# Gathering the first slot of key rows one block earlier, into the buffers of the tap products and the gate weights, in a two-layer perceiver kernel

## The chip, the cores and the metric

The kernel runs on one core of a Trainium2 chip. The metric is the device time of one execution in microseconds (us); the median of the runs is compared.

## The reference, cut to what matters

128 query rows `x` (width 256) pass two layers. Layer 0 is a cross-attention over 12,544 context rows with 4 heads, a gated delta rule with 12 heads, and a mixture of 8 experts (top 1). Layer 1 is a second cross-attention over the same context with 16 heads, a linear attention and another mixture (top 2). Each stage adds to `x`, and each starts with a layer norm:

```python
x = x + _L0_xattn_ref(_layernorm(x), ctx_1024, mask, ...)
x = x + _L0_attn_ref(_layernorm(x), ...)          # gated delta rule
x = x + _L0_ffn_ref(_layernorm(x), ...)           # experts, top 1
x = x + _L1_xattn_ref(_layernorm(x), ctx_1024, ...)
x = x + _L1_attn_ref(_layernorm(x), ...)
x = x + _L1_ffn_ref(_layernorm(x), ...)
```

In the second cross-attention scores = (q + bias) k^T / 4 for each of 16 heads of width 16, then a softmax over all context rows, then the product with v. Its keys and values depend on the context alone, not on `x`.

## The kernel before

The program is three blocks, each of which ends with a barrier of all engines. Block 1 (to 448 us) is the first cross-attention over 14 chunks of 896 context rows; beside it the kernel already computes the keys and values of layer 1 for every chunk and stores them in HBM (`kscr`, in two halves of 512 and 384 columns, and `vscr`). Block 2 (448 to 537 us) is the delta rule: `Wc`, `Wg`, `Wo` are its weights, `vpair` (seen as `vp`) holds the products of its convolution taps, ScalarE writes them in `products`, GpSimd adds them up in `add_taps`, and each group of them that is done raises the semaphore `convp` (5 groups). `gate` multiplies by `Wg`, and ScalarE's reading of the product raises `sg` (3 groups). Block 3 (from 537 us) is the experts `moe0`, the second cross-attention (`second_sync`, `second_tensor`, `second_vector`, ...), the linear attention and the last experts `moe1`.

The second cross-attention reads a chunk of keys from SBUF tiles `krows`, a ring of three slots for each of the two halves, 96 partitions wide (and three rows of ones). `gather(sp, c, half)` fills slot `c % 3` with four DMAs from SyncE's queue (L1654). The first two gathers, for chunk 0, stand at the end of the loads that `moe0` issues (`l1_loads`, L1675), behind the weights `lraw`, `dec`, `bg`, `bv1`; `fetch_values` (L1661) and the gathers of chunk 1 (L1785) come behind them.

What TensorE does in block 3 is written out by hand. After the query is ready, four calls of `pick_rows` (L2001) build the query rows in the layout of the keys, and ScalarE copies them (L2131, semaphore `qpicked`). The list `PRO1` is the prologue: 16 scores of chunk 0 and 7 of chunk 1 (`score`, L1904: two matmuls, 512 and 384 columns), among them 14 `late_values` (L1992). The first score waits for both halves of slot 0:

```python
if h == 0:
    for half in range(2):
        pe.wait_ge(S(f"krows{half}_{r}"), 16 * GPARTS * (c // R1 + 1))
```

VectorE takes the maximum of each score (`largest`, L2061) and so frees one of two pairs of PSUM banks, so that a score waits for the maximum of the score two places ahead (`sm_free`). Then comes the loop over 14 chunks, which interleaves transposed scores (L1948), values (L1961) and the scores of the chunk after (L1904); the negated maxima go into the query rows by three small DMAs per chunk (`rows`, L1777).

Of the kernel before, what the change touches and what calls it, by code (L numbers as in the profile page):

```python
# [17 lines left out]
F32 = mybir.dt.float32  # L18
BF16 = mybir.dt.bfloat16
# [5 lines left out]
P = 128  # L25
D = 256
DC = D // P
# [4 lines left out]
HW = (HT[0] * P, HT[1] * P)  # L32
# [6 lines left out]
TWO_ONES = 1.0 + 127.0 / 65536.0  # L39
# [3 lines left out]
H1, D1 = 16, 16  # L43
# [5 lines left out]
KROWS = NJ * D1  # L49
KONES = KROWS + 3  # L50
VW = H1 * (D1 + 1) + D1 - 1

NH, DK, DV = 12, 64, 128
# [3 lines left out]
TAPS = 4  # L57
GH = 4
NG = NH // GH
# [7 lines left out]
def build(nc, a, out):  # L67
# [4 lines left out]
    def S(name):  # L72

        if name not in sems:
            sems[name] = nc.alloc_semaphore(name)
        return sems[name]
# [31 lines left out]
    def sb(st, name, shape, dt=F32):  # L108
        return st.enter_context(nc.sbuf_tensor(name, shape, dt))
# [9 lines left out]
    with ctx:  # L119
        psum = ctx.enter_context(nc.psum_tensor("bank", [P, 8, 512], F32))  # L120
        bank = [psum[:, i, :] for i in range(8)]
# [3 lines left out]
        keep = ctx.enter_context(ExitStack())  # L125
# [60 lines left out]

        home = sb(keep, "home", [P, DC * CB * P])
        eT0 = home[:, 0:DC * E * D].rearrange("p (k e d) -> p k e d", k=DC, e=E)
        gw = ExitStack()
        Wc = home[:].rearrange("p (k o) -> p k o", k=DC)  # L190
        Wg = sb(gw, "Wg", [P, DC, NH * DV])
        Wo = sb(gw, "Wo", [P, NH, D])
        Wgb = sb(gw, "Wgb", [P, DC, 2 * NH])
        convw = sb(gw, "convw", [P, CB, TAPS])
        gbias = sb(gw, "gbias", [P, 2 * NH])
        nA = sb(gw, "nA", [P, NH])
        gnw = sb(gw, "gnw", [P, DV])
        vpair = sb(gw, "vpair", [P, TAPS * 2 * GH * P])

        def load_later_weights(eng, part):  # L200

# [709 lines left out]
            return tile[:, hb(g)].rearrange("p (j e) t -> p e j t", e=2)  # L911

        spent = []
        STILL = ("rms", "og", "on", "oT_psum", "oT", "ew0_in", "e0T_psum", "e0T", "x2_psum", "x2", "vscr_mid", "moe0rw_in")

        with nc.Block(no_gpsimd_drain=True) as block:
            @block.sync
            def _(sp):
                sp.dma_start(ew[:], a["L0_ffn_expert_w"].rearrange("e (c p) d -> p (e c) d", p=P)).then_inc(S("ew0_in"), 16)
                sp.dma_start(rwmoe0[:], a["L0_ffn_router_w"]).then_inc(S("moe0rw_in"), 16)  # L920
                sp.wait_ge(S("v1mid"), CT)
                sp.dma_start(vscr[NCH - 2].rearrange("p t w -> p (t w)"),
                             v1s[:, 0].rearrange("p t w -> p (t w)")).then_inc(S("vscr_mid"), 16)
                sp.wait_ge(S("vscr_mid"), 16)

            @block.vector
            def _(dve):
# [701 lines left out]
        bv1 = sb(xb, "bv1", [P, D])  # L1629
        rd1 = sb(xb, "rd1", [P, H1])  # L1630
        l1 = ExitStack()
        R1, PR = 3, 8
        krows = [sb(l1, f"krows{half}", [KONES, R1, H1, HW[half]], BF16) for half in range(2)]
        v1 = sb(l1, "v1", [P, R1, CT, VW])
        mx1 = sb(l1, "mx1", [P, 2, H1])
        run1 = sb(l1, "run1", [P, 2, H1])
# [7 lines left out]
        HB = P // D1  # L1644
        pickhome = v1[:, 2].rearrange("p t w -> p (t w)")[:, 0:3 * HB * KROWS // 2]
        picks = pickhome.bitcast(BF16).rearrange("p (l k r) -> p l k r", l=HB, k=3)

        GPARTS = 4

        def gather(sp, c, half):  # L1650

            for part in range(GPARTS):
                heads = slice(part * H1 // GPARTS, (part + 1) * H1 // GPARTS)
                sp.dma_start(krows[half][0:KROWS, c % R1, heads].rearrange("r h m -> r (h m)"),  # L1654
                             kscr[half][c].rearrange("j (d h) b m -> (j d) (h b) m", d=D1)[:, heads].rearrange("r h m -> r (h m)")
                             ).then_inc(S(f"krows{half}_{c % R1}"), 16)

        def fetch_values(sp, c):

# [4 lines left out]
        def l1_loads(sp):  # L1664
            o = (0, 6, 8, 10)
            for k, name in enumerate(("L1_attn_Wqkv", "L1_attn_Wout", "L1_attn_Wgate")):
                sp.dma_start(lraw[:, o[k]:o[k + 1]], wcols(a[name], o[k + 1] - o[k])).then_inc(S("lraw_in"), 16)
            dp = a["L1_attn_decay_param"].rearrange("(c h) -> c h", c=DC)
            for c in range(DC):
                sp.dma_start(dec[:, c:c + 1], dp[c].unsqueeze(1).to_broadcast([HL // DC, DL]).unsqueeze(2)  # L1670
                             ).then_inc(S("dec_in"), 16)
            sp.dma_start(bg[:], a["L1_attn_bgate"].rearrange("(c p) -> p c", c=DC),
                         allow_slow_non_contiguous=True).then_inc(S("bg_in"), 16)
            sp.dma_start(bv1[:], a["L1_xattn_bv"].partition_broadcast(P)).then_inc(S("bv1_in"), 16)
            gather(sp, 0, 0)  # L1675
            gather(sp, 0, 1)
            fetch_values(sp, 0)

        def l1_clears(pool):
# [88 lines left out]
        def krow(h):  # L1768

            return h % (P // D1) * DC + h // (P // D1)  # L1770
# [55 lines left out]
        def second_gpsimd(pool):  # L1826
# [35 lines left out]
            value_ones(pool, 2)  # L1862
            pool.wait_ge(S("v1late_ones"), 4)
            pool.wait_ge(S("q3"), 3)
            def ones_rows(half, slots):
                pool.memset(krows[half][KROWS:KONES, slots].rearrange("p s h m -> p (s h m)").bitcast(F32),
                            TWO_ONES).then_inc(S("krows_ones"), 1)
                pool.wait_ge(S("krows_ones"), nth("krows_ones"))

            ones_rows(0, slice(0, 1))  # L1870
            ones_rows(1, slice(0, 1))
            ones_rows(0, slice(1, R1))
            for c in range(NCH):
                maximum(c)
                if c:
                    rescale(c - 1)
                else:
                    pool.wait_ge(S("dm1"), 1)
                    ones_rows(1, slice(1, R1))
                    block_mask()  # L1880
            rescale(NCH - 1)

        def second_tensor(pe):
# [12 lines left out]
            def score(c, h):  # L1896

                r, b = c % R1, sm_bank(("S", c, h))
# [3 lines that stand above are left out]
                sm_free(("S", c, h))  # L1902
                for half in range(2):
                    ins = pe.matmul(bank[b + half][:, 0:HW[half]], qrows[0:KROWS, 0, h, :],  # L1904
                                    krows[half][0:KROWS, r, krow(h), :], start=True, stop=True)
                ins.then_inc(S("sm1"), 1)

            def turn_maximum(c):
# [23 lines left out]
            def scores(c, u):  # L1932

                t, j, g = u // 4, u % 4, UNITS * c + u
                if u == 0:
                    if c == 0:
                        pe.wait_ge(S("krows_ones"), 2)
                    if c == 1:
                        pe.wait_ge(S("krows_ones"), 4)
                        pe.wait_ge(S("qrows_copy"), 16)  # L1940
                    pe.wait_ge(S(f"mrow1_{c % 2}"), 48 * (c // 2 + 1))
                if some(g - 2):
                    pe.wait_ge(S("exp1"), g - 2)
                half = t // HT[0]
                cols = slice((t - half * HT[0]) * P, (t - half * HT[0] + 1) * P)
                for i in range(GH):
                    h = GH * j + i
                    ins = pe.matmul(bank[ST1[g % 3]][:, i * P:(i + 1) * P], krows[half][:, c % R1, krow(h), cols],  # L1948
                                    qrows[:, c % 2, h, :], start=True, stop=True)
                ins.then_inc(S("st1"), 1)  # L1950

# [438 lines left out]
```

## Time and profile before

| | us |
|---|---|
| median of 3 runs | 920.16 (918.53 to 923.98) |
| profiled execution, its own time | 920.66 |
| its span | 918.9 |
| PE busy | 888.6 (97% of the span) |
| VectorE busy | 702.5 (76%) |
| ScalarE busy | 487.3 (53%) |
| GpSimd busy | 301.2 (33%) |
| mean granted TensorE clock | 0.995 of full |

PE is TensorE's matmuls, PEld its weight loads, DVE VectorE, ACT ScalarE, POOL GpSimd, SPq the DMA issues of SyncE. The profiled execution's time is 1.8 us above its span and 0.5 us above the median. PE busy is the share of time with a matmul in flight and does not say that the matmuls run at full rate; the granted clock says at which rate they may run.

### The profile page before, as it was taken

The numbers are of one execution on the slowest core, as the hardware profiler recorded it, in microseconds if no ns is written. First come the engines' busy times: TensorE is split into PE (matmuls) and PEld (weight loads), VectorE is DVE, ScalarE is ACT, GpSimd is POOL, SyncE is SP. The second block draws the span as 40 slices with busy tenths as digits, with TensorE's granted clock in tenths as the row PEclk, the third lists the DMA queues.
The fourth block names the chain that finished last, engine by engine and source line by source line (L and its number), as shares of the span: only waits on it lengthen the run. The fifth ranks groups of instructions, "written<-read, shape, count | busy, mean of one in ns | idle before, by whom it ended". The sixth has DMA issues, their size and how long they took to land. (4 is left out here: it accounts for less than half of the span.)

```text
span 918.9 us, 21566 instructions
## 1 busy us (share of the span) xinstructions
PE 888.6 (97%) x8228; PEld 573.2 (62%) x8228; DVE 702.5 (76%) x1218; ACT 487.3 (53%) x1158; POOL 301.2 (33%) x439
## 2 busy tenths in 40 slices
PE   8999999999999999999899988999999999999898
PEld 5444554555455545665779866667776776776675
DVE  3499888987988898999488655878887888887426
ACT  2543554355345534545297323466766766666753
POOL 5563355336434643566018224500011100000000
PEclk9999999999999999999999998999999999999999
DMA  9467856573556356531410049596666665776100
GB/s 171 173 185 208 261 181 182 142 211 133 141 150 196 104 138 193 165 120 70 145 46 1 2 127 237 153 290 177 185 168 168 168 169 168 181 193 176 47 4 6
DMA packets 115080, 136.35 MB, mean 148 GB/s; under 512 B 65720, under 2 KB 86992, under 8 KB 114992
## 3 DMA queue, kind: packets, MB, share of 16 engines
q1 hardware_dynamic: 111280, 134.23, 52.1%
q10 hardware_dynamic: 3712, 0.92, 0.7%
q8 instruction: 59, 0.97, 0.5%
q14 instruction: 29, 0.24, 0.1%
HBM read 81.48 MB, written 53.07 MB: 146 GB/s over the span
## 5 line engine op out<-in xcount | busy, mean ns | idle before, releaser
L2061 DVE TENSOR_REDUCE mx<-bank 128x1 f32<-128x896 f32 x224 | 233.7, 1085 | 52.6 <-PE bank L1904 49.3
L2122 ACT ACTIVATE p<-bank 128x512 f32<-128x512 f32 x392 | 202.4, 602 | 94.1 <-PE bank L1948 93.9
L721 DVE STREAM_TRANSPOSE ew<-sc 32x896 f32<-32x896 f32 x208 | 229.4, 1103 | 27.7 <-ACT sc L805 20.2
L580 PE MATMUL bank<-Wv,ctxT 128*128 128x512 f32 (+1 forms) x308 | 133.7, 574 | 0.0
L1948 PE MATMUL bank<-home,krows 99*128 99x128 bf16 x1568 | 123.5, 220 | 5.9 <-DMA home<-n3T 2.9
L1904 PE MATMUL bank<-krows,home 96*128 96x512 bf16 x448 | 123.3, 357 | 5.1 <-DMA krows<-kscr 3.7
L1948 PEld LDWEIGHTS bank<-home,krows 99*128 99x128 bf16 x1568 | 99.4, 97 | 43.7 <-issue 8.2
L1961 PE MATMUL bank<-p,v 128*32 128x128 f32 x3136 | 106.8, 276 | 0.9 <-issue 0.9
L1961 PEld LDWEIGHTS bank<-p,v 128*32 128x32 f32 x3136 | 80.1, 109 | 31.3 <-ACT p L2122 27.8
L580 PEld LDWEIGHTS bank<-Wv,ctxT 128*128 128x128 f32 x308 | 58.3, 190 | 65.3 <-issue 58.4
L457 POOL CAST kt<-kf 128x512 bf16<-128x512 f32 (+1 forms) x56 | 31.3, 558 | 202.0 <-ACT kf L777 201.9
L1830 POOL TENSOR_SCALAR neg<-run 128x16 f32<-128x16 f32 x14 | 3.6, 256 | 249.1 <-DVE run L2076 249.1
L777 ACT ACTIVATE kf<-bank,b 128x512 f32<-128x512 f32 (+1 forms) x56 | 35.5, 634 | 86.6 <-PE bank L560 85.6
L560 PE MATMUL bank<-ctxT,WTk 128*128 128x384 f32 (+1 forms) x176 | 75.6, 552 | 0.0
L805 ACT ACTIVATE sc<-sc,neg 128x448 f32<-128x448 f32 x112 | 74.3, 667 | 0.0
L542 PE MATMUL bank<-ctxT,Wk 128*128 128x448 f32 x176 | 70.9, 546 | 0.9 <-ACT kT L765 0.9
L668 DVE CUSTOM_DVE_ANT_0 sc<-bank,pen 128x448 f32<-128x448 f32 x112 | 63.9, 620 | 4.2 <-issue 4.0
L792 ACT COPY v<-bank 128x256 f32<-128x256 f32 x77 | 28.7, 373 | 66.9 <-PE bank L580 66.9
L765 ACT COPY kT<-bank 128x448 f32<-128x448 f32 x56 | 29.7, 532 | 61.6 <-PE bank L542 61.6
L461 POOL TENSOR_TENSOR kf<-kf,kt 128x512 f32<-128x512 f32 (+1 forms) x56 | 58.3, 1041 | 4.4
L463 POOL TENSOR_TENSOR kt<-kf,kt 128x512 bf16<-128x512 f32 (+1 forms) x56 | 58.1, 1038 | 4.4
L459 POOL TENSOR_TENSOR kt<-kf,kt 128x512 bf16<-128x512 f32 (+1 forms) x56 | 58.0, 1036 | 4.5
(339 smaller groups left out, 1155.1 us busy)
## 6 DMA issues: line engine op xcount, KB each, us to landing
krows<-kscr SPq DMA_DIRECT2D x56, 384.0 KB, 6.2
krows<-kscr SPq DMA_DIRECT2D x56, 288.0 KB, 8.9
vscr<-vpair SPq DMA_DIRECT2D x12, 1004.5 KB, 4.0
kscr<-kt SPq DMA_DIRECT2D x14, 768.0 KB, 3.6
kscr<-kt SPq DMA_DIRECT2D x14, 576.0 KB, 5.1
v<-vscr SPq DMA_DIRECT2D x14, 574.0 KB, 10.8
kscr<-kt SPq DMA_DIRECT2D x14, 512.0 KB, 4.5
ctxB<-ctx SPq DMA_DIRECT2D x56, 112.0 KB, 3.9
```

Of the source, the lines that this page charges most:

```text
L461: pool.tensor_tensor(f, f, kh[:, 0, b], ALU.subtract).then_inc(S("kr1"), 1)
L542: ins = pe.matmul(bank[kv_bank(op, s)][:, 0:HCH], Wk0[:, i, b * P:(b + 1) * P], turned_context(c)[:, i, half * HCH:(half + 1) * HCH], star ...
L560: ins = pe.matmul(bank[kv_bank(op, s)][:, 0:HW[half]], WTk[:, i, b * P:(b + 1) * P], turned_context(c)[:, i, HO[half]:HO[half] + HW[half]] ...
L580: ins = pe.matmul(bank[kv_bank(op, s)][:, 0:w * D], turned_context(c)[:, i, k * P:(k + 1) * P], Wv01[:, i, 0:w].rearrange("p w o -> p (w o)"),
L668: dve.tensor_tensor_reduce(out=sc0[:, s, h, half * HCH:(half + 1) * HCH], in0=bank[SX[k % 4]][:, 0:HCH], in1=pen0[:, half * HCH:(half + 1) ...
L721: dve.transpose(pT0[j * SQ:(j + 1) * SQ, :, :, i * SQ:(i + 1) * SQ].rearrange("m t h q -> m h t q"), rows[:, j]).then_inc(S("turn0"), 1)
L805: act.activation(sc0[:, s, h, cols], sc0[:, s, h, cols], ACT.Exp, bias=neg0[:, h:h + 1], accum_out=den0[:, s, h, half:half + 1]).then_inc( ...
L1904: ins = pe.matmul(bank[b + half][:, 0:HW[half]], qrows[0:KROWS, 0, h, :], krows[half][0:KROWS, r, krow(h), :], start=True, stop=True)
L1948: ins = pe.matmul(bank[ST1[g % 3]][:, i * P:(i + 1) * P], krows[half][:, c % R1, krow(h), cols], qrows[:, c % 2, h, :], start=True, stop=True)
L1961: ins = pe.matmul(bank[OT1][32 * i:32 * i + 32, j * P:(j + 1) * P], v1[:, c % R1, t, h * (D1 + 1):h * (D1 + 1) + 32], p1[:, g % PR, i * P: ...
L2061: dve.tensor_reduce(mx1[:, c % 2, h:h + 1], psum[:, b:b + 2, :].rearrange("p b n -> p (b n)")[:, 0:CH], AX.X, ALU.max).then_inc(S("smread1 ...
L2122: act.activation(p1[:, g % PR, :], bank[ST1[g % 3]][:], ACT.Exp).then_inc(S("exp1"), 1)
```

## The change

`Wg` and `vpair` move to the stack `keep`, so that they stay in place to the end. Slot 0 of the ring is no tile of its own any more: half 0 is the memory of `vpair`, half 1 that of `Wg` (both fit exactly), and the other two slots are the tiles `krest`. The gathers of chunk 0 are issued by SyncE in block 2: half 1 once `sg` has reached 3 (`Wg` has been read for the last time), half 0 once `convp` has reached 5 (`vpair` has been read for the last time). They are gone from `l1_loads`. The semaphores of slot 0, `sg` and `convp` are left out of the clearing at the end of block 2. The rest of the diff gives the slots as a list instead of an index.

```diff
--- before.py
+++ after.py
@@ -186,16 +186,16 @@
 
         home = sb(keep, "home", [P, DC * CB * P])
         eT0 = home[:, 0:DC * E * D].rearrange("p (k e d) -> p k e d", k=DC, e=E)
+        Wg = sb(keep, "Wg", [P, DC, NH * DV])
+        vpair = sb(keep, "vpair", [P, TAPS * 2 * GH * P])
         gw = ExitStack()
         Wc = home[:].rearrange("p (k o) -> p k o", k=DC)
-        Wg = sb(gw, "Wg", [P, DC, NH * DV])
         Wo = sb(gw, "Wo", [P, NH, D])
         Wgb = sb(gw, "Wgb", [P, DC, 2 * NH])
         convw = sb(gw, "convw", [P, CB, TAPS])
         gbias = sb(gw, "gbias", [P, 2 * NH])
         nA = sb(gw, "nA", [P, NH])
         gnw = sb(gw, "gnw", [P, DV])
-        vpair = sb(gw, "vpair", [P, TAPS * 2 * GH * P])
 
         def load_later_weights(eng, part):
 
@@ -911,7 +911,19 @@
             return tile[:, hb(g)].rearrange("p (j e) t -> p e j t", e=2)
 
         spent = []
-        STILL = ("rms", "og", "on", "oT_psum", "oT", "ew0_in", "e0T_psum", "e0T", "x2_psum", "x2", "vscr_mid", "moe0rw_in")
+        STILL = ("rms", "og", "on", "oT_psum", "oT", "ew0_in", "e0T_psum", "e0T", "x2_psum", "x2", "vscr_mid", "moe0rw_in", "sg", "convp", "krows0_0", "krows1_0")
+
+        R1, GPARTS = 3, 4
+        krows = [[vpair[0:KONES].bitcast(BF16).rearrange("r (h m) -> r h m", h=H1)],
+                 [Wg[0:KONES].rearrange("r c n -> r (c n)").bitcast(BF16).rearrange("r (h m) -> r h m", h=H1)]]
+
+        def gather(sp, c, half):
+
+            for part in range(GPARTS):
+                heads = slice(part * H1 // GPARTS, (part + 1) * H1 // GPARTS)
+                sp.dma_start(krows[half][c % R1][0:KROWS, heads].rearrange("r h m -> r (h m)"),
+                             kscr[half][c].rearrange("j (d h) b m -> (j d) (h b) m", d=D1)[:, heads].rearrange("r h m -> r (h m)")
+                             ).then_inc(S(f"krows{half}_{c % R1}"), 16)
 
         with nc.Block(no_gpsimd_drain=True) as block:
             @block.sync
@@ -922,6 +934,10 @@
                 sp.dma_start(vscr[NCH - 2].rearrange("p t w -> p (t w)"),
                              v1s[:, 0].rearrange("p t w -> p (t w)")).then_inc(S("vscr_mid"), 16)
                 sp.wait_ge(S("vscr_mid"), 16)
+                sp.wait_ge(S("sg"), NG)
+                gather(sp, 0, 1)
+                sp.wait_ge(S("convp"), 5)
+                gather(sp, 0, 0)
 
             @block.vector
             def _(dve):
@@ -1629,8 +1645,10 @@
         bv1 = sb(xb, "bv1", [P, D])
         rd1 = sb(xb, "rd1", [P, H1])
         l1 = ExitStack()
-        R1, PR = 3, 8
-        krows = [sb(l1, f"krows{half}", [KONES, R1, H1, HW[half]], BF16) for half in range(2)]
+        PR = 8
+        krest = [sb(l1, f"krest{half}", [KONES, R1 - 1, H1, HW[half]], BF16) for half in range(2)]
+        for half in range(2):
+            krows[half].extend(krest[half][:, r] for r in range(R1 - 1))
         v1 = sb(l1, "v1", [P, R1, CT, VW])
         mx1 = sb(l1, "mx1", [P, 2, H1])
         run1 = sb(l1, "run1", [P, 2, H1])
@@ -1645,16 +1663,6 @@
         pickhome = v1[:, 2].rearrange("p t w -> p (t w)")[:, 0:3 * HB * KROWS // 2]
         picks = pickhome.bitcast(BF16).rearrange("p (l k r) -> p l k r", l=HB, k=3)
 
-        GPARTS = 4
-
-        def gather(sp, c, half):
-
-            for part in range(GPARTS):
-                heads = slice(part * H1 // GPARTS, (part + 1) * H1 // GPARTS)
-                sp.dma_start(krows[half][0:KROWS, c % R1, heads].rearrange("r h m -> r (h m)"),
-                             kscr[half][c].rearrange("j (d h) b m -> (j d) (h b) m", d=D1)[:, heads].rearrange("r h m -> r (h m)")
-                             ).then_inc(S(f"krows{half}_{c % R1}"), 16)
-
         def fetch_values(sp, c):
 
             for tiles in (slice(0, HT[0]), slice(HT[0], CT)):
@@ -1672,8 +1680,6 @@
             sp.dma_start(bg[:], a["L1_attn_bgate"].rearrange("(c p) -> p c", c=DC),
                          allow_slow_non_contiguous=True).then_inc(S("bg_in"), 16)
             sp.dma_start(bv1[:], a["L1_xattn_bv"].partition_broadcast(P)).then_inc(S("bv1_in"), 16)
-            gather(sp, 0, 0)
-            gather(sp, 0, 1)
             fetch_values(sp, 0)
 
         def l1_clears(pool):
@@ -1862,21 +1868,20 @@
             value_ones(pool, 2)
             pool.wait_ge(S("v1late_ones"), 4)
             pool.wait_ge(S("q3"), 3)
-            def ones_rows(half, slots):
-                pool.memset(krows[half][KROWS:KONES, slots].rearrange("p s h m -> p (s h m)").bitcast(F32),
-                            TWO_ONES).then_inc(S("krows_ones"), 1)
+            def ones_rows(rows):
+                pool.memset(rows.bitcast(F32), TWO_ONES).then_inc(S("krows_ones"), 1)
                 pool.wait_ge(S("krows_ones"), nth("krows_ones"))
 
-            ones_rows(0, slice(0, 1))
-            ones_rows(1, slice(0, 1))
-            ones_rows(0, slice(1, R1))
+            for half in range(2):
+                ones_rows(krows[half][0][KROWS:KONES].rearrange("p h m -> p (h m)"))
+            ones_rows(krest[0][KROWS:KONES].rearrange("p s h m -> p (s h m)"))
             for c in range(NCH):
                 maximum(c)
                 if c:
                     rescale(c - 1)
                 else:
                     pool.wait_ge(S("dm1"), 1)
-                    ones_rows(1, slice(1, R1))
+                    ones_rows(krest[1][KROWS:KONES].rearrange("p s h m -> p (s h m)"))
                     block_mask()
             rescale(NCH - 1)
 
@@ -1902,7 +1907,7 @@
                 sm_free(("S", c, h))
                 for half in range(2):
                     ins = pe.matmul(bank[b + half][:, 0:HW[half]], qrows[0:KROWS, 0, h, :],
-                                    krows[half][0:KROWS, r, krow(h), :], start=True, stop=True)
+                                    krows[half][r][0:KROWS, krow(h), :], start=True, stop=True)
                 ins.then_inc(S("sm1"), 1)
 
             def turn_maximum(c):
@@ -1945,7 +1950,7 @@
                 cols = slice((t - half * HT[0]) * P, (t - half * HT[0] + 1) * P)
                 for i in range(GH):
                     h = GH * j + i
-                    ins = pe.matmul(bank[ST1[g % 3]][:, i * P:(i + 1) * P], krows[half][:, c % R1, krow(h), cols],
+                    ins = pe.matmul(bank[ST1[g % 3]][:, i * P:(i + 1) * P], krows[half][c % R1][:, krow(h), cols],
                                     qrows[:, c % 2, h, :], start=True, stop=True)
                 ins.then_inc(S("st1"), 1)
```

The order of instructions on SyncE, in block 2 (L916 and L928 are the branch at its end, L922 and L934 the store of the values of chunk 12 from `vpair`). Before:

```order
L919 DMA ew<-L_ffn_expert_w 128x16x256
L920 DMA rwmoe<-L_ffn_router_w 8x256
L922 DMA vscr<-vpair 128x2009 [waits v1mid]
L916 UNCONDITIONAL_BRANCH [waits vscr_mid]
L2331 UNCONDITIONAL_BRANCH [waits barrier_Pool_Activation_PE_DVE_SP_release]
```

and with the change:

```order
L931 DMA ew<-L_ffn_expert_w 128x16x256
L932 DMA rwmoe<-L_ffn_router_w 8x256
L934 DMA vscr<-vpair 128x2009 [waits v1mid]
L924 DMA Wg<-kscr 96x1536 [waits sg,vscr_mid]
L924 DMA Wg<-kscr 96x1536 x3
L924 DMA vpair<-kscr 96x2048 [waits convp]
L924 DMA vpair<-kscr 96x2048 x3
L928 UNCONDITIONAL_BRANCH
L2336 UNCONDITIONAL_BRANCH [waits barrier_Pool_Activation_PE_DVE_SP_release]
```

Eight gathers now stand between the store and the barrier. The same queue at the start of block 3, before:

```order
L1674 DMA bv<-L_xattn_bv 128x256
L1654 DMA krows<-kscr 96x2048 x4
L1654 DMA krows<-kscr 96x1536 x4
L1661 DMA v<-vscr 128x1148
L1661 DMA v<-vscr 128x861
L1654 DMA krows<-kscr 96x2048 x4
L1654 DMA krows<-kscr 96x1536 x4
L1788 DMA home<-home 96x2048
```

and with the change:

```order
L1682 DMA bv<-L_xattn_bv 128x256
L1669 DMA v<-vscr 128x1148
L1669 DMA v<-vscr 128x861
L924 DMA krest<-kscr 96x2048 x4
L924 DMA krest<-kscr 96x1536 x4
L1794 DMA home<-home 96x2048
```

The eight gathers of chunk 0 are gone from there, and those of chunk 1 follow the first values. On TensorE no row moves. Around the first score (semaphore numbers are reused, so that `ln0_var` stands for `qpicked`), before:

```order
L2001 MATMUL bank<-home,v 96x256 [waits x1_psum]
L2001 MATMUL bank<-home,v 96x256 x5
L1904 MATMUL bank<-krows,home 128x512 [waits krows0_0,krows1_0,ln0_var,x1_psum]
L1904 MATMUL bank<-krows,home 128x384
L2001 MATMUL bank<-home,v 96x256 [waits x1_psum]
```

and with the change:

```order
L2006 MATMUL bank<-home,v 96x256 [waits x1_psum]
L2006 MATMUL bank<-home,v 96x256 x5
L1909 MATMUL bank<-vpair,home 128x512 [waits krows0_0,krows1_0,ln0_var,x1_psum]
L1909 MATMUL bank<-Wg,home 128x384
L2006 MATMUL bank<-home,v 96x256 [waits x1_psum]
```

The first score waits for the same semaphores and reads the other tiles.

## Rows read from the trace of the kernel before

**Rows 1.** Chain that ended last, piece by piece, 542 to 574 us: start, length, what.

```profile
542.59 2.98 SPq L1654
...
548.07 12.27 DMA krows<-kscr
...
561.38 1.28 PE bank L2001 x6
...
566.08 1.73 PE bank L1992 x8
567.81 0.38 PE bank L1904 x2
...
570.71 3.10 DVE mx L2061 x3
```

**Rows 2.** Timeline of SyncE's queue, the gathers of chunk 0.

```profile
541.65 7.15 SPq L1654 DMA_DIRECT2D krows<-kscr  x8
```

**Rows 3.** Timeline of block 3, TensorE and ScalarE, in brackets the idle time before.

```profile
537.00 0.26 PE L1500 MATMUL bank<-ident,rwmoe 8*128 8x8 f32 x2 [1.08 <-PEq L916]
555.27 1.48 PE L2001 MATMUL bank<-home,v 128*96 128x256 bf16 x12 [0.27 <-issue]
556.14 1.24 ACT L2131 CAST home<-bank 96x512 bf16<-96x512 f32 x2 [0.30 <-PE bank L2001]
560.47 0.91 PE L1904 MATMUL bank<-krows,home 96*128 96x512 bf16 x2 [3.72 <-DMA krows<-kscr]
567.64 0.54 PE L1904 MATMUL bank<-krows,home 96*128 96x512 bf16 x2
```

**Rows 4.** Four stretches: busy time by engine (count), granted clock, DMA share, GB/s.

```profile
552.00:556.80 4.80, 4.49 (x40) 4.02 (x38) 2.14 (x6) 3.13 (x7) 0.00 (x0) 1.00 1.05 242
556.80:560.40 3.60, 0.00 (x0) 0.00 (x0) 0.00 (x0) 0.57 (x1) 0.00 (x0) 0.81 1.02 266
560.40:564.40 4.00, 3.93 (x16) 3.01 (x17) 2.05 (x2) 0.58 (x1) 0.00 (x0) 0.50 1.07 231
564.40:570.00 5.60, 5.60 (x26) 3.99 (x25) 3.85 (x5) 1.70 (x4) 5.07 (x4) 0.87 1.02 246
```

**Rows 5.** Timeline of VectorE: the maximum of the score at 567.64.

```profile
568.23 1.09 DVE L2061 TENSOR_REDUCE mx<-bank 128x1 f32<-128x896 f32 x1 [0.67 <-PE bank L1904]
```

**Rows 6.** Timeline of block 2: store landed, last gate, last tap sum, the barrier's end.

```profile
468.61 0.21 POOL L1395 MEMSET vpair<- 128x24 f32 x3 [14.71 <-DMA vscr<-vpair]
478.13 0.58 ACT L1099 ACTIVATE sg<-bank 128x512 f32<-128x512 f32 x1
504.12 1.27 POOL L1406 TENSOR_TENSOR cv<-cv,vpair 128x512 f32<-128x512 f32 x1
536.96 0.13 POOL L1489 MEMSET ordermoe<- 128x1 f32 x2 [7.48 <-POOLq L916]
```

**Rows 7.** ScalarE by form, 505 to 537 us, then 610 to 880 us.

```profile
L1178 ACT ACTIVATE Z<-bank 128x512 f32<-128x512 f32 x3 | 1.8, 598 | 3.3 <-PE bank L1200 3.3
L2122 ACT ACTIVATE p<-bank 128x512 f32<-128x512 f32 x354 | 183.0, 602 | 86.3 <-PE bank L1948 86.2
```

**Rows 8.** Two stretches: busy time by engine, granted clock, DMA share, GB/s.

```profile
500.00:536.90 36.90, 34.10 (x283) 31.28 (x281) 22.22 (x39) 13.09 (x27) 10.90 (x8) 1.00 0.00 1
610.00:700.00 90.00, 90.00 (x1592) 64.46 (x1590) 76.00 (x81) 62.87 (x128) 7.57 (x28) 1.00 0.67 183
```

**Rows 9.** Chain that ended last in the loop over chunks.

```profile
702.89 0.88 issue
```

**Rows 10.** The page's DMA issues: KB each, median us to landing.

```profile
krows<-kscr SPq DMA_DIRECT2D x56, 384.0 KB, 6.2
krows<-kscr SPq DMA_DIRECT2D x56, 288.0 KB, 8.9
```

**Rows 11.** Timeline of TensorE: the loop's first scores, and the first that wait for a DMA.

```profile
588.20 0.83 PE L1948 MATMUL bank<-home,krows 99*128 99x128 bf16 x12
...
609.49 0.61 PE L1948 MATMUL bank<-home,krows 99*128 99x128 bf16 x8 [1.27 <-DMA home<-n3T]
```

## The prediction

> **What bounds the kernel now.** I began with the page: PE is busy for 97% of the span, so only a place where TensorE stands still or runs slowly can give anything back. The chain that ended last shows one such place at the start of the second cross-attention: it runs through SyncE's issues of the gathers, then 12.27 us of one gather in flight, and comes back to TensorE at 560.47, with the first score [rows 1, 3]. The timeline of SyncE says why that gather is late: all eight DMAs of chunk 0 are issued from 541.65 to 548.80, behind the weights of the layer [rows 2], and one of those issues takes 2.98 us itself [rows 1]. TensorE and ScalarE show what is missed: TensorE is through with the first two query picks (12 matmuls) at 555.27 + 1.48 = 556.75, the first of two casts that the score needs ends at 556.14 + 1.24 / 2 = 556.76, and the score starts after an idle 3.72 us put down to the gather [rows 3].
>
> The second thing to see is the clock. Up to 556.80 it is 1.00 (2.4 GHz); within the idle stretch it falls (mean 0.81), from 560.40 to 564.40 it is 0.50 (1.2 GHz), and from 564.40 to 570 it is 0.87 in the mean [rows 4]. What TensorE did before it fell was nothing, for want of the gather. So the late gather costs the idle time and then some microseconds at half speed: a score takes 0.91 us at 560.47 and 0.54 us at 567.64 [rows 3].
>
> **What the change removes: the wait.** The eight DMAs leave the queue of block 3. They are issued in block 2, half 1 after the last read of the gate weights (478.13 + 0.58 = 478.7) and half 0 after the last tap sum (504.12 + 1.27 = 505.4) [rows 6]. They carry 4 x 384 + 4 x 288 = 2,688 KB [rows 10], or 2.75 MB; at the 231 to 266 GB/s that the crowded stretch shows [rows 4] that is 10 to 12 us of the DMA engines, 4.7 us for half 1 and 6.3 us for half 0. Half 0 is then in place near 514, over 40 us before its reader. The first score can start at 556.80 instead of 560.47: 3.67 us.
>
> **The half-speed stretch.** Without an idle stretch the clock has no cause to fall. I rebuild the pieces between the first score and the first late values, at full clock. Two matmuls of a score take 0.38 us of the chain [rows 1]; six of a pick take half of 1.28, 0.64 us, as 12 of them took about 1.28 plus the tail in [rows 3]. A maximum starts 568.23 - 567.64 = 0.59 us after its score and lasts 1.09 [rows 3, 5].
> - Score 0 at 556.80, pick 3 at 557.18, score 1 at 557.82, pick 4 at 558.20, score 2 at 558.84 (it needs maximum 0, which ends at 558.48).
> - Score 3 needs maximum 1. That starts at 558.48 and ends at 559.55, so score 3 runs from 559.60 to 559.98.
> - The late values start at 559.98. In the trace they start at 566.08 [rows 1]: 6.10 us.
>
> So the clock is worth 6.10 - 3.67 = 2.4 us. Its bounds: 0 if the clock falls all the same, 2.8 if score 3 need not wait (4 x 0.38 + 2 x 0.64 = 2.80 against 5.61 us). From 566 on two late values take 1.73 us, full rate [rows 1], and from 570.71 the maxima run back to back [rows 1], fed by the same scores in the same order, so everything behind moves by 6.1 us as a block. VectorE does not become the new bound, because its work before 570.71 moves too.
>
> The Trainium skill (TensorE: Matmul & The Clock Gate, "What's actually happening") says that low clock is the default and activity releases it, and that the gate's view of activity runs freely, not in step with the program; by it the same idle gap costs half-speed work in one execution and less in another. The trace agrees that the gap and the fall go together, but it is one execution.
>
> **What the change adds.** *SyncE* waits for `sg` and then for `convp` before it reaches the barrier. Nothing stands behind it in block 2: its store was done at 468.6, when GpSimd is released by it, and the others reach the barrier at 536.96 [rows 6], 31 us after the second wait is met. Eight issues cost it some 7 us [rows 2], all inside those 31. Cost 0; if that cover were gone, the last issue would hold the barrier by its own length.
>
> *The delta rule* gets DMA traffic where it had none (share 0.00 [rows 8]). Does an engine slow down beside it? ScalarE's 128x512 square takes 598 ns with no traffic and the loop's 128x512 exponential 602 ns at a share of 0.67 [rows 7, 8]. I take 0. The page lists two queues of instruction fetches beside the kernel's own; the loop shows a stall of 0.88 us, put down to no engine, beside traffic [rows 9]. Two of these in the delta rule, 1.8 us, are the upper bound. The Trainium skill (DMA: Bandwidth & Descriptors, "Queues, rings and completion order") has each DMA engine take turns between queues packet by packet, so that a fetch would wait for little; by it the bound is nearer 0 than 1.8. No run here shows the fetches' own waits.
>
> *Block 3's queue* is shorter: the first values and chunk 1's gathers are issued some 7 us earlier and land earlier. Chunk 1 is first read by the 17th score, at least 16 maxima of over 1 us behind the first, so that gives nothing, and nothing else is queued behind it but the copy that waits for the picks. The slot's address, the wider life of two tiles and the list in place of an index add no instruction: 0.
>
> *The loop* starts 6.1 us earlier with the same distances between its DMAs and their triggers. Of those transfers one held TensorE, 1.27 us at 609.49 [rows 11]. I take 0 and keep plus or minus 1.3 us.
>
> **Sum.** -3.67 - 2.43 + 0 + 0 = -6.1 us, with ends of -0.6 (nothing from the clock, 1.8 lost to fetches, 1.3 in the loop: 3.67 - 3.1) and -7.8 (3.67 + 2.8 + 1.3). Against the profiled execution's own 920.66 that is 914.6; the median is 0.5 us lower, so I give 920.16 - 6.1 = **914.1 us**, 0.66% less. A measurement of this kernel can tell about 0.5%, 4.6 us, from no change.
>
> **The rivals.**
> - *Only the idle time.* In the executions that are timed the clock did not fall behind the gap, or falls now at another place. Gain 3.67 us: 916.5. For it: the profiled execution is 0.5 us above the median, as if it had paid for something. Against: 0.50 for a whole 4 us right behind the gap [rows 4]. Chance 0.17. The rule of the Trainium skill's page TensorE: Matmul & The Clock Gate, named above, would bring this about in some executions and not in others.
> - *The loop gives some back.* Its transfers meet other traffic and show two waits more like the one of 1.27 us [rows 11]: gain 3.5, 916.6. Chance 0.10. The reverse, that this wait goes too (its transfer ran in a crowded stretch), gives 912.8. Chance 0.04.
> - *Slower: the gathers slow the delta rule.* Its matrices go from TensorE to VectorE and back with no slack (PE 34.1 of 36.9 us [rows 8]), so each slower operation is paid. With the 11 us of traffic on top, operations that take x times as long cost 11 (x - 1): it eats the 6.1 us from x = 1.55, and at x = 2 the kernel is slower by 4.9 us, 925.1. Against it: 598 and 602 ns [rows 7]. Chance 0.04.
> - *It doesn't do what it says*: the first score still waits, for something that the gather hid (the casts, the weights' transposes). Both are through by 556.8 in the trace [rows 3]. 920.2, chance 0.03.
>
> **Numbers.** The forecast has 0.62, at 913 to 915.2 by itself. The range of 911.8 to 918.3 takes in the clock rival and the loop's, up to a gain of 1.9 us, which is the clock rival with all 1.8 us of the fetches; it leaves out the slower case, the empty one, the two or three bad bounds at once and the spread of the medians beyond, 0.15 to 0.2 together. Faster by over 0.5%: nearly all of the forecast (0.59), the 0.04 of the lucky loop, 0.03 of the two partial rivals: 0.66. Slower: 0.04. Within 0.5%: 0.30.
>
> **What would show it.** In the changed profile: SyncE's gathers at about 479 and 505; block 2 as long as before (448 to 537 us); no idle time at TensorE's first score, which starts about 19.8 us behind the first matmul of block 3 instead of 560.47 - 537.00 = 23.5 [rows 3]; a clock of 1.00 from 552 to 570; late values at about 560.0; the first scores of the loop at about 582.1 instead of 588.20 [rows 11], and the end 6.1 us earlier. A delta rule that is longer by more than 1 us, an idle gap at the first score, or a clock under 1 behind it would each break a step.

## The result and the profile after

| | before | after |
|---|---|---|
| median of 10 runs, us | 919.49 (918.12 to 923.98) | 914.24 (913.03 to 918.12) |
| profiled execution, its own time, us | 920.66 | 913.46 |
| its span, us | 918.9 | 911.7 |
| mean granted TensorE clock | 0.995 | 0.999 |

The change makes the kernel 5.25 us faster; the ratio is 0.9945, with a 95% interval of 0.9927 to 0.9963. The forecast was 6.1 us, to 914.1. The profiled spans differ by more, 7.2 us. A good part of what follows is about why these three numbers differ.

The stretches that [rows 4] showed, in the changed kernel (busy time of PE, PEld, DVE, ACT, POOL with counts, then granted clock, DMA share, GB/s):

```profile
552.00:556.80 4.80, 4.53 (x40) 4.15 (x39) 2.14 (x6) 3.08 (x6) 0.00 (x0) 1.00 1.00 216
556.80:560.40 3.60, 3.24 (x22) 2.31 (x22) 2.78 (x3) 1.79 (x4) 1.04 (x3) 1.00 0.93 232
560.40:564.40 4.00, 4.00 (x20) 3.10 (x20) 3.01 (x4) 1.12 (x3) 3.94 (x2) 1.00 0.43 133
564.40:570.00 5.60, 5.45 (x26) 3.46 (x25) 5.45 (x6) 1.49 (x4) 5.54 (x2) 1.00 0.03 7
```

TensorE worked none of the 3.6 us behind 556.80 before; now it works 3.24 of them. The clock is 1.00 in all four rows; in the last three it was 0.81, 0.50 and 0.87. The DMA engines, full until 570 before, are through by about 563.

TensorE's timeline, which answers to [rows 3] and the loop's start of [rows 11]:

```profile
555.40 1.48 PE L2006 MATMUL bank<-home,v 128*96 128x256 bf16 x12 [0.27 <-issue]
556.95 0.38 PE L1909 MATMUL bank<-vpair,home 96*128 96x512 bf16 x1
...
559.85 0.38 PE L1909 MATMUL bank<-vpair,home 96*128 96x512 bf16 x1 [0.30 <-ACT home L2136]
...
582.52 0.83 PE L1953 MATMUL bank<-home,vpair 99*128 99x128 bf16 x12
603.35 0.61 PE L1953 MATMUL bank<-home,krest 99*128 99x128 bf16 x8 [0.74 <-DMA home<-n3T]
```

The first score reads `vpair` at 556.95 with no wait. The fourth waits 0.30 us. The trace puts that down to ScalarE's cast of the fourth pick, but by the program the fourth score needs only the first two picks. VectorE's second maximum ends at about 557.62 + 4.08 / 2 = 559.66 (half of four equal maxima), and that is the wait of the prediction's list:

```profile
557.62 4.08 DVE L2066 TENSOR_REDUCE mx<-bank 128x1 f32<-128x896 f32 x4 [2.32 <-PE bank L1909]
562.54 1.09 DVE L2066 TENSOR_REDUCE mx<-bank 128x1 f32<-128x896 f32 x1 [0.84 <-PE bank L1909]
```

The chain that ended last no longer touches SyncE here; its first late values:

```profile
559.21 0.59 ACT home L2136
559.85 0.54 PE bank L1909 x2
560.39 1.73 PE bank L1997 x8
```

Late values at 560.39 instead of 566.08 [rows 1] and the loop at 582.52 instead of 588.20 [rows 11]: 5.7 us in the one profile against the other. The other 1.5 of the 7.2 us arose later, in the loop.

SyncE's queue in block 2, and ScalarE's square there, which answers to [rows 7]:

```profile
478.92 1.73 SPq L924 DMA_DIRECT2D Wg<-kscr  x4
505.50 1.71 SPq L924 DMA_DIRECT2D vpair<-kscr  x4
537.07 0.36 SPq L1494 DMA_DIRECT2D rbmoe<-L_ffn_router_b  x1
```

```profile
L1194 ACT ACTIVATE Z<-bank 128x512 f32<-128x512 f32 x3 | 1.8, 597 | 3.3 <-PE bank L1216 3.3
```

The gathers are issued where they were expected, the eight take 3.4 us of SyncE instead of 7.2, and block 3 starts 0.12 us later than before (537.12 against 537.00).

### The profile page after: what moved, and what is told of

It reads as the page before. It is cut to its first block and busy times, and to the rows that moved or that the text cites. A ratio compares the mean times of both kernels' runs of the same rounds, so it can differ in the third digit from the quotient of the medians.

```text
span 911.7 us, 21566 instructions
## 1 busy us (share of the span) xinstructions
PE 886.0 (97%) x8228; PEld 571.6 (63%) x8228; DVE 702.2 (77%) x1218; ACT 487.0 (53%) x1158; POOL 300.7 (33%) x439
## 5 line engine op out<-in xcount | busy, mean ns | idle before, releaser
L1953 PE MATMUL bank<-home,krest 99*128 99x128 bf16 x1008 | 79.2, 220 | 3.0 <-ACT p L2127 1.7
L1953 PEld LDWEIGHTS bank<-home,krest 99*128 99x128 bf16 x1008 | 63.9, 97 | 27.0 <-issue 5.3
L1909 PE MATMUL bank<-krest,home 96*128 96x512 bf16 (+1 forms) x288 | 78.4, 354 | 1.3 <-DVE mx L2066 1.2
```

## The experiments

Times are medians of several runs; the kernel before ran beside each of three groups of experiments (medians 919.5 to 919.9 us), and each ratio is to the one beside it. In the excerpts of code `...` stands for lines left out.

**The changed kernel again**, beside the next three. 

> The changed kernel once more, beside the others. Theory: 5 to 6 us faster than before, block 2 unchanged, first score without a wait, loop of the same length as before within 1.5 us.

915.09 us, ratio 0.9947 (0.9927 to 0.9968). A third set of runs, below, gives 914.87 (0.9955, 0.9933 to 0.9977). The gain repeats: the medians differ by 5.25, 4.8 and 4.7 us. From the loop's first transposed scores to the end of the span the three profiles take 329.2, 330.6 and 329.6 us.

**Idle matmuls in the gap of the kernel before.**

```diff
+            spin(pe, 3, 15)
             for n, op in enumerate(PRO1):
```

> The kernel before, with 15 idle matmuls (30 passes of about 0.11 us, 3.4 us) between the second pick and the first score, so that TensorE is busy while it waits for the gather. Theory (gain = idle time 3.7 us + half clock 2.4 us): the wait stays, the clock stays at 1.00, the late values follow the first score by 3.0 to 3.3 us instead of 5.6, and the kernel is 2.0 to 2.6 us faster than before. Rival (the clock is no part of it, only the idle time is): same time as before within 0.3 us.

919.77 us, ratio 0.9998 (0.9975 to 1.0021): no gain in the median where 2.0 to 2.6 us were expected, though the interval reaches to 2.3 us faster. In the profiled execution the clock stays (0.999 over the span) and the late values follow the first score by 3.3 us, as the theory says:

```profile
556.64 3.51 PE L167 MATMUL bank<-ident 128*128 128x128 f32 x30
559.99 0.54 PE L1904 MATMUL bank<-krows,home 96*128 96x512 bf16 x2
```

But the score shows no wait for the gather: the idle matmuls set its start. The last gather is issued at 548.1 and lands at most 11.6 us later, by 559.7, against 12.27 us [rows 1]; so the matmuls add some 0.3 us to this gap. The runs go from 915.7 to 923.95 us, and that spread is hardly the clock's: the mean clock is 0.998 to 1.000 in all twelve, where the kernel before beside them goes down to 0.992. That the gap is longer in some executions and is lengthened by the matmuls in others would explain it, but no run shows the gap of an execution that was not profiled. The run doesn't separate clock and wait; a wait of fixed length was needed.

**The kernel before again.** 

> The kernel before, once more, for a second look at its gather. Theory (the landing of slot 0 varies from execution to execution, and with it the wait and the clock): the first score does not start at 560.5 again but anywhere from 557 to 564, and the rest of the prologue is as long as the clock behind the gap makes it. Rival (the landing is fixed, and the runs differ in the loop alone): first score at 560.2 to 560.8, late values 5.6 us behind it.

920.59 us (ratio 1.0008, 0.9987 to 1.0029). TensorE's first score and two of the stretches:

```profile
559.80 0.54 PE L1904 MATMUL bank<-krows,home 96*128 96x512 bf16 x2 [2.73 <-DMA krows<-kscr]
```

```profile
556.80:560.40 3.60, 0.87 (x7) 0.48 (x6) 0.00 (x0) 0.82 (x2) 0.00 (x0) 1.00 1.06 278
560.40:564.40 4.00, 3.70 (x25) 2.83 (x24) 3.92 (x4) 1.41 (x3) 2.18 (x3) 1.00 1.03 220
```

Here the wait is 2.73 us, not 3.72, and the clock does not fall. Late values follow the first score by 3.3 us, not 5.6, and the loop starts at 585.38, not 588.20. Both values lie inside the 557 to 564 that were expected, and a few profiles don't show how far the landing varies; but it does vary. Counted from the block's first matmul the last gather is in at 23.3 us in the first profile of before, 22.4 in this one and by 22.7 in the run with idle matmuls. The two profiles also give the price of the lost clock in the prologue: from the first score to the loop's start 27.73 us with it lost, 25.58 with it kept, 2.15 us.

**A gap of fixed length, idle or busy.** Both are the changed kernel with a wait for VectorE in place of the wait for the gather; the second has idle matmuls in it (the line with `spin`, which the first leaves out). `held` is a small tile for results that nothing reads.

```diff
+            spin(pe, 3, 15)
+            pe.wait_ge(S("held"), 5)
             for n, op in enumerate(PRO1):
...
             query()
             dve.wait_ge(S("bg_in"), 16)
+            for i in range(5):
+                dve.tensor_reduce(held[:, i:i + 1], ctxT0[:, 0, :],
+                                  AX.X, ALU.max).then_inc(S("held"), 1)
```

> The changed kernel, with a wait of fixed length in place of the gather's: VectorE first does five maxima over 128x896 that nothing uses (5.2 us, from 555.3), and the first score waits for them. So TensorE is idle from about 556.8 to 560.6 in every execution. Theory (an idle gap of that length costs itself and then up to 2.4 us at half clock): first score 3.7 us later, clock 0.50 behind it in the profile, 4.5 to 6.1 us slower than the changed kernel in the median, so within 1 us of the kernel before. Rival (only the idle time counts): 3.7 us slower than the changed kernel. Third (the loop takes the delay up): 0 to 1 us.

> The same wait of fixed length, with 15 idle matmuls (3.4 us) ahead of the first score, which end before the fifth maximum does. Theory: first score as late as in the run with the idle gap (3.7 us), clock 1.00 behind it, late values 3.1 us behind the first score, and 1 to 2.4 us faster than the run with the idle gap. Rival (the clock costs nothing, since VectorE's maxima set the pace): the same time as with the idle gap, within 0.5 us.

922.0 us idle (ratio 1.0035, 1.0014 to 1.0056) and 919.14 us busy (0.9998, 0.9981 to 1.0014). The idle one's timeline and stretches:

```profile
560.50 0.38 PE L1910 MATMUL bank<-vpair,home 96*128 96x512 bf16 x1 [3.61 <-DVE held L2106]
...
562.23 1.49 PE L2007 MATMUL bank<-home,v 128*96 128x256 bf16 x6
```

```profile
556.80:560.40 3.60, 0.09 (x1) 0.00 (x0) 3.60 (x4) 0.64 (x2) 0.00 (x0) 1.00 0.89 228
560.40:564.40 4.00, 3.90 (x19) 2.82 (x20) 2.19 (x3) 1.16 (x2) 0.50 (x3) 0.65 0.10 38
564.40:570.00 5.60, 5.57 (x26) 3.83 (x25) 4.47 (x5) 1.49 (x4) 5.54 (x2) 0.95 0.24 70
```

and the busy one's:

```profile
560.48 0.39 PE L1910 MATMUL bank<-vpair,home 96*128 96x512 bf16 x1 [0.22 <-DVE held L2107]
```

```profile
556.80:560.40 3.60, 3.46 (x32) 3.27 (x30) 3.60 (x4) 0.66 (x2) 0.00 (x0) 1.00 0.97 237
560.40:564.40 4.00, 3.68 (x24) 2.73 (x25) 3.35 (x5) 1.16 (x2) 1.49 (x3) 1.00 0.17 64
```

The first score is equally late (560.50, 560.48), 3.5 us behind the changed kernel's. With the gap busy the clock stays and the loop starts at 586.01, idle at 587.30. In the medians the busy gap costs 4.2 us against the changed kernel's 914.95 (all its 33 runs; none of them stood beside these two) and the idle one another 2.9 us, 7.0 in all. The idle one is slower than expected, slower even than the kernel before.

So a gap of this length costs its own length, 3.5 us in the profile and 4.2 in the medians, and it costs more idle than busy. How much more is known less well. The two ratios' intervals just touch, so 2.9 us stands for anything from almost nothing to some 5 (by resampling the 12 and 12 runs). The profile of the idle gap has only 1.3 us of it at the loop's start (587.30 against 586.01), where the clock was low for a shorter time than in the first profile of before (0.65 and 0.95 against 0.81, 0.50 and 0.87, which cost 2.15 us); the rest arose in the loop, where its clock fell a second time (0.65 from 610 to 614 us). The kernel before pays less than wait and clock together (4.8 us in the median against 7.0). Its gap was shorter in the second profile and the clock stayed there, so it is likely that it does not pay both in every execution.

**Half 1 alone early.** Half 0 is gathered in block 3 again, at its old place in the queue.

```diff
                 sp.wait_ge(S("sg"), NG)
                 gather(sp, 0, 1)
-                sp.wait_ge(S("convp"), 5)
-                gather(sp, 0, 0)
...
+            gather(sp, 0, 0)
             fetch_values(sp, 0)
```

> The change for half 1 alone: its four gathers in block 2, into the gate weights; half 0 is gathered in block 3 at its old place, before the first values. Theory (the gather was late because of the bytes ahead of it and beside it in the queue, of which 1.2 of 4.2 MB are gone): half 0 lands at 553 to 557, and nearly all the gain is there, 4.5 to 6 us. Rival (the last gather is late by a fixed chain of issue and flight, whatever lies beside it): half 0 lands at 544 + 12 = 556 or later, a gain of 2 to 4 us.

914.70 us (7 runs), ratio 0.9930 (0.9904 to 0.9955): all of the gain. Half 0 is issued behind the weights and still in time:

```profile
541.91 4.68 SPq L924 DMA_DIRECT2D vpair<-kscr  x4
```

```profile
557.07 0.38 PE L1908 MATMUL bank<-vpair,home 96*128 96x512 bf16 x1
```

Its last DMA is issued at 546.2, 1.9 us earlier than the last of the eight before, and lands at most 10.3 us later instead of 12.3, so by 556.5. That is half a microsecond ahead of the score, which shows no wait. A fixed flight of 12 us would have ended at 558.2, so that rival is refuted, and taking 1.2 MB out of the queue is enough.

**The kernel before, later transfers held back.**

```diff
             gather(sp, 0, 1)
+            for half in range(2):
+                sp.wait_ge(S(f"krows{half}_0"), 16 * GPARTS)
             fetch_values(sp, 0)
```

> The kernel before, but SyncE waits until chunk 0's keys have landed before it issues the first values and chunk 1's gathers. Theory (these later transfers take a share of the engines and delay the eight gathers): lraw, bv1 and eight gathers are 4.2 MB, at 245 GB/s through at 555 to 557 instead of 560.3, a gain of 3.5 to 6 us with no buffer changed. Rival (the transfers are served in order, later ones cost nothing): landing stays at 560, gain 0, or a loss if the values or chunk 1 come late now.

918.31 us, ratio 0.9982 (0.9963 to 1.0002). In the profile the wait is less than half as long:

```profile
557.80 0.54 PE L1906 MATMUL bank<-krows,home 96*128 96x512 bf16 x2 [1.51 <-DMA krows<-kscr]
```

The last gather is in 21.1 us behind the block's first matmul, against 23.3, 22.4 and 22.7 in the three profiles with the old queue: 1.3 to 2.2 us earlier. Part of that is SyncE, which issued the eight in 6.6 us instead of 7.1; the longest flight is 10.6 us instead of 12.3, 11.3 and 11.6. So transfers issued later probably take a share from earlier ones, 0.7 to 1.7 us of flight, but one profile stands against a spread of 1 us. What is left of the wait has the queue ahead as its likely cause, which this run doesn't test. The gain in time, 1.6 us, is at the edge of what the runs can tell, and below the 3.5 to 6 expected.

**More traffic in the delta rule.** Half 1 gathered five times and half 0 three times, each behind the other; `gather` takes the name of the semaphore that it raises, which the excerpt leaves out.

```diff
                 sp.wait_ge(S("sg"), NG)
+                for i in range(4):
+                    gather(sp, 0, 1, "extra1")
+                    sp.wait_ge(S("extra1"), 64 * (i + 1))
                 gather(sp, 0, 1)
                 sp.wait_ge(S("convp"), 5)
+                for i in range(2):
+                    gather(sp, 0, 0, "extra0")
+                    sp.wait_ge(S("extra0"), 64 * (i + 1))
                 gather(sp, 0, 0)
```

> The changed kernel with the gathers of the delta rule repeated, one after the other: half 1 five times, half 0 three times, 10.6 MB instead of 2.75 MB, from 479 to about 525. The data are the same each time. Theory (traffic costs the delta rule nothing): block 2 ends at 537.1 plus or minus 0.3, the time is that of the changed kernel within 0.7 us. Rival (traffic slows the engines or their instruction fetches, and part of the forecast gain was lost there): block 2 longer by 1 us or more, 1 to 4 us slower than the changed kernel.

> The run with 10.6 MB of gathers in the delta rule again, since its median was 1.4 us above the changed kernel's of another call while its block 2 was as long. Theory (traffic there is free, the difference was the loop's chance): median within 0.7 us of the changed kernel's beside it, block 2 ends at 537.1 to 537.3. Rival (heavy traffic costs something in part of the executions): 1 to 2 us slower again.

Beside the second of these runs stood the changed kernel: 

> The changed kernel a third time, beside the run with three to five times the traffic. Both theories: 914 to 915.5.

916.48 and 917.35 us (ratios 0.9965, 0.995 to 0.9981, and 0.9968, 0.9947 to 0.9989), the changed kernel beside it 914.87. The stretches of the first, and the same stretch of the changed kernel with its 2.75 MB:

```profile
479.00:505.50 26.50, 26.50 (x244) 26.38 (x244) 21.49 (x36) 19.83 (x69) 23.20 (x18) 1.00 0.66 180
505.50:537.00 31.50, 28.77 (x234) 26.07 (x230) 17.88 (x32) 10.70 (x19) 7.18 (x6) 1.00 0.74 189
```

```profile
479.00:505.50 26.50, 26.50 (x244) 26.38 (x244) 21.48 (x36) 19.74 (x69) 23.25 (x18) 1.00 0.18 46
```

TensorE, VectorE and GpSimd are busy for the same time at a DMA share of 0.66 as at 0.18, and the block ends at the same place: its successor's first matmul comes at 537.18 and 536.83 us, against 536.57 to 537.12 in three profiles of the changed kernel. ScalarE's 128x512 squares from 505 to 537 us, at a share of 0.74, take the 597 ns that they take in the changed kernel:

```profile
L1200 ACT ACTIVATE Z<-bank 128x512 f32<-128x512 f32 x3 | 1.8, 597 | 3.3 <-PE bank L1222 3.3
```

So in both profiles the delta rule paid nothing. Yet the median of the 24 runs is 916.85, 1.9 us above that of the changed kernel's 33. In the first set it is 1.5 us above, in the second 2.5, where the intervals of the two ratios overlap; so the loss is likely, and neither set alone would show it. Both profiles lose their time in the loop, which lasts 333.9 us in each; the last section shows where. Why heavy traffic before it should lead there stays open; the 2.75 MB of the change cannot be told from none by these runs.

**One late value moved ahead of the fourth score**, in the changed kernel.

```diff
-                if n == 3:
-                    late_values(0)
-                    late_values(1)
+                if n in (2, 3):
+                    late_values(n - 2)
```

> The changed kernel with the first late value moved from behind the fourth score to ahead of it, into the 0.3 us in which the fourth score waits for a maximum. Theory (the prologue is bound by VectorE's maxima now, which stand idle 0.84 us ahead of the fifth): the fifth score comes about 0.3 us earlier and the idle time ahead of the fifth maximum is under 0.3 us, gain 0.3 to 0.8 us, hardly to be told. Rival (bound elsewhere, by the chain of the maxima's rows): loop start at the same time, gain 0.

915.07 us, ratio 0.9945 (0.993 to 0.996). VectorE's gap ahead of the fifth maximum shrinks from 0.84 to 0.15 us and the loop starts at 582.06, 0.46 us earlier:

```profile
562.08 1.09 DVE L2065 TENSOR_REDUCE mx<-bank 128x1 f32<-128x896 f32 x1 [0.15 <-PE bank L1909]
```

In the time it can't be seen. **With half 1 alone early as well:** 

> Half 1 alone gathered early (only the gate weights live on) and the first late value ahead of the fourth score. Theory (half the early gather gives all of the gain, the moved value 0.46 us more): first score without a wait, loop start at 582.1 to 582.3, median 914 to 915, no slower than the full change. Rival (half 0 lands just too late in many executions): 1 to 3 us slower than the full change.

914.11 us, ratio 0.9937 (0.9913 to 0.996), the loop at 581.86. This variant beats the kernel before and is level with the changed one, with one tile less kept alive and no second wait in SyncE.

## Why the prediction was right, and where a step was off

- *What bounded the kernel, and that the wait goes.* Right: gathers at 478.9 and 505.5 (said: 479 and 505), first score at 19.8 us behind the block's first matmul (556.95 - 537.12; said: 19.8), no wait.
- *The rebuilt prologue.* Late values were put at 559.98 and came at 560.39. Of the 0.41 us, 0.12 is the block's later start. Three more pieces were put too short: the first maximum starts 0.67 us behind its score, not 0.59; the fourth score starts about 0.2 us behind the maximum that frees its bank, not 0.05; and it takes 0.54 us of the chain behind its wait, not 0.38. The maxima, at 1.02 us each, give a little back. The term was 6.10 us; the two profiles give 5.7.
- *The step that was off in size: the sum.* It took one execution's gap (3.72 us) and one execution's clock (0.50) for the median's. The median gained 5.25, 4.8 and 4.7 us in three sets of runs. The second profile of before has a gap of 2.73 us and a clock of 1.00. The rival "only the idle time" named this, and the truth lies between it (3.67) and the forecast. The mean clocks of the runs show a mixture over executions: of 98 runs of before beside the experiments, the 18 with 0.999 or more take 917.9 us in the mean, the 22 such runs of the changed kernel 914.3. That is 3.6 us among executions that kept their clock, the size of the wait alone; the rest of the gain presumably lies in the executions of before that lost it. The mechanism itself is right: with a gap of fixed length the wait costs 3.5 to 4.2 us, and an idle gap costs more than a busy one. The term for the clock, 2.43 us, was sized well for the profile that it was read from (2.15), and too high for the median.
- *The delta rule at 0.* Right for this change in every profile; block 3 starts 0.12 us later than in the first profile of before, and three to five times the traffic leaves the block as long. The slower rival (operations slowed by traffic) is refuted for that block: 597 ns at a DMA share of 0.74 against 598 at none. But heavy traffic there seems to cost some 1.9 us elsewhere, which was not expected.
- *Chunk 1's earlier gathers give nothing.* Right: nothing else moved in the prologue.
- *The loop at plus or minus 1.3 us.* Too narrow. The loop and what follows it take 330.7 us in the first profile of before and 329.2 in the changed kernel's; over all fourteen profiles, most of them of altered kernels, they take from 328.4 to 333.9.

## What to carry to other kernels

A wait for a transfer at a fixed place can cost a different amount in each execution; one profile gives one draw of it, and its clock is another. Read the mean granted clock of every run beside the times before a term is taken from one trace, and measure a disputed gap with a wait of fixed length. And before buffers are shared to move a whole transfer, try to move half of it: here 1.2 MB less in the queue was enough.

## What the runs showed that was not expected

**The same loss has a second place, in the loop.** The first scores of chunk 1 wait for three small DMAs behind a crowded queue [rows 11]. In three profiles of the changed kernel that wait was 0.64 to 0.89 us. In two of the experiments it was 1.76 us to the hundredth, and only one of them lost the clock. The second run with heavy traffic:

```profile
604.13 1.00 PE L1959 MATMUL bank<-home,krest 99*128 99x128 bf16 x8 [1.76 <-DMA home<-n3T]
...
607.41 1.94 PE L1972 MATMUL bank<-p,v 128*32 128x128 f32 x32
...
624.16 1.08 PE L1972 MATMUL bank<-p,v 128*32 128x128 f32 x32
```

```profile
602.00:606.00 4.00, 2.24 (x30) 1.56 (x19) 0.83 (x2) 1.08 (x2) 0.00 (x0) 0.77 0.68 181
606.00:610.00 4.00, 4.00 (x49) 2.80 (x48) 2.69 (x3) 1.17 (x3) 0.00 (x0) 0.50 1.00 235
```

and the last experiment (half 1 early, late value moved):

```profile
603.63 0.61 PE L1952 MATMUL bank<-home,krest 99*128 99x128 bf16 x8 [1.76 <-DMA home<-n3T]
...
620.53 1.08 PE L1965 MATMUL bank<-p,v 128*32 128x128 f32 x32
```

```profile
602.00:606.00 4.00, 2.37 (x44) 1.81 (x47) 1.59 (x3) 1.95 (x4) 0.00 (x0) 1.00 0.96 256
606.00:610.00 4.00, 4.00 (x82) 3.00 (x71) 3.44 (x5) 2.18 (x5) 0.00 (x0) 1.00 1.01 258
```

Behind an equal wait the same 32 value matmuls take 1.94 us in the one, 1.08 being usual. From that first score to the sixth group of value matmuls behind it the one takes 20.03 us and the other 16.90; these 3.1 us go with the lost clock. The loops last 333.9 and 329.4 us. The clock also fell there in the run with the moved value (0.70 in the second of these stretches, loop 333.7 us), in the first with heavy traffic (0.57, 333.9) and, some 4 us later, in the one with the idle gap. This agrees with the Trainium skill (TensorE: Matmul & The Clock Gate, "What's actually happening"), by which the gate's view of activity runs freely, not in step with the program: whether an idle piece of given length costs half-speed work is then a matter of when it falls. No run here separates that from what else differs between these executions.

The loop varies for another reason as well. In the runs with half 1 alone early and with the later transfers held back the clock is 1.00 throughout the loop, which still lasts 332.2 and 332.9 us. In the second of them TensorE stands still for 2.9 us ahead of three groups of value matmuls, for nothing that the profile shows (total, times, longest):

```profile
PE bank L1963 <- issue: 2.9, 3, 1.4
```

In the first profile of the changed kernel there is 0.2 us of this in one place. It is the kind of stall that the prediction bounded at 1.8 us for the delta rule [rows 9]; that block was no longer, and here it appears in the loop. What it is stays open. The spread that is left in the changed kernel goes with the clock as well: of its 33 runs, those with a mean clock of 0.998 or less (11) took 915.6 to 919.8 us, the others 912.6 to 917.0.

**The landing that the change takes off the path was probably the larger source of spread.** The mean clock of before's runs goes down to 0.992. The 20 of 98 with 0.995 or less took 922.4 us in the mean, those of 0.999 and more 917.9. The changed kernel has one run of 0.995 or less in 33.
